# Attention kernel: diagonal blocks share PSUM banks, and the order of the work is laid out anew

## The reference, cut to what matters

```python
scores = jnp.einsum('bhqd,bhkd->bhqk', q, k) * scale
causal = jnp.tril(jnp.ones((t, t), dtype=bool))
scores = jnp.where(causal[None, None], scores, -jnp.inf)
att = jax.nn.softmax(scores, axis=-1)
y = jnp.einsum('bhqk,bhkd->bhqd', att, v)
```

## Time and profile before

| | |
|---|---|
| median of three runs | 1970.04 us (1965.76 to 1972.16) |
| the profiled execution | 1966.68 us |
| its span, first to last instruction | 1964.9 us |
| mean granted TensorE clock | 0.979 |
| PE busy | 1860.7 us, 95% |
| DVE busy | 1697.8 us, 86% |
| ACT busy | 1611.4 us, 82% |
| POOL busy | 554.1 us, 28% |

### The profile page before, as it was taken

How to read it: one execution, slowest core, us unless ns; L and a number is a source line. 1 busy time by engine, 2 the same in 40 slices (tenths; PEclk the granted TensorE clock), 3 DMA queues, 4 the chain that set the end, 5 groups by cost and what they waited for, 6 DMA issues and landing times.

```text
span 1964.9 us, 42229 instructions
## 1 busy us (share of the span) xinstructions
PE 1860.7 (95%) x13881; PEld 694.6 (35%) x13881; DVE 1697.8 (86%) x4770; ACT 1611.4 (82%) x2108; POOL 554.1 (28%) x712
## 2 busy tenths in 40 slices
PE   6899999999789999999999999999999999999998
PEld 6455565555322222222232322223232222223223
DVE  5699999999888898989899998989999899989861
ACT  2467666765269999999999999999999999999994
POOL 0112111221313424241442424143242414334211
PEclk8899999999769999999999999999999999999999
DMA  4133323335421404042341414133131414314012
GB/s 172 35 92 101 104 82 89 101 101 110 108 66 29 65 21 63 21 62 37 62 65 42 62 43 83 34 65 63 44 62 40 83 29 73 59 43 67 29 36 81
DMA packets 160327, 129.04 MB, mean 66 GB/s; under 512 B 95344, under 2 KB 144752, under 8 KB 159768
## 3 DMA queue, kind: packets, MB, share of 16 engines
q1 hardware_dynamic: 160152, 126.88, 30.0%
HBM read 74.60 MB, written 42.98 MB: 60 GB/s over the span
## 4 chain that ended last, share of the span: by engine, by line
PE 48%; ACT 16%; DVE 3%; issue 3%; DMA 2%; SPq 2%; POOL 1%; ACTq 0%; POOLq 0%; DVEq 0%
PE pv L1511 20%; ACT prob L1304 12%; PE st L1498 11%; PE sm L1477 10%; PE sm L1448 3%; ACT excess L1297 3%; PE st L1486 3%; DMA scratch_i<-inverse 1%; DVE pm L1383 1%; DVE sm L1379 1%; PE sm L1472 1%; SPq L913 1%; DVE sm L1368 0%; ACT Y L1287 0%; DMA Yc<-Y 0%
## 5 line engine op out<-in xcount | busy, mean ns | idle before, releaser
L1304 ACT ACTIVATE prob<-st 128x1024 f32<-128x1024 f32 (+3 forms) x1280 | 1078.3, 900 | 77.8 <-PE st L1498 66.1
L1511 PE MATMUL pv<-prob,V 128*32 128x512 f32 (+3 forms) x5120 | 594.1, 541 | 0.4 <-POOL prob L1261 0.2
L1368 DVE CUSTOM_DVE_ANT_0 sm<-sm,mask 128x128 f32<-128x128 f32 (+3 forms) x1024 | 491.6, 510 | 62.5 <-PE sm L1477 50.3
L1477 PE MATMUL sm<-K,Q 48*128 48x512 f16 (+3 forms) x2112 | 522.7, 349 | 16.3 <-DVE pm L1383 4.3
L1498 PE MATMUL st<-Q,K 50*128 50x512 f16 (+3 forms) x2560 | 484.1, 353 | 28.5 <-ACT prob L1304 21.1
L1261 POOL TENSOR_SCALAR_AFFINE_SELECT prob<-prob 128x256 f32<-128x256 f32 x512 | 206.1, 409 | 932.3 <-ACT prob L1304 926.5
L1383 DVE TENSOR_REDUCE pm<-sm 128x1 f32<-128x512 f32 x640 | 416.8, 683 | 24.3 <-PE sm L1477 22.1
L1379 DVE CUSTOM_DVE_ANT_0 sm<-sm,excess 128x512 f32<-128x512 f32 x448 | 311.1, 716 | 33.7 <-PE sm L1477 25.8
L1477 PEld LDWEIGHTS sm<-K,Q 48*128 48x128 f16 x2112 | 167.5, 94 | 324.9 <-DVE pm L1383 158.6
L1498 PEld LDWEIGHTS st<-Q,K 50*128 50x128 f16 x2560 | 126.6, 93 | 421.3 <-ACT prob L1304 299.6
L1297 ACT ACTIVATE excess<-st 128x1024 f32<-128x1024 f32 x219 | 224.8, 1026 | 17.6 <-PE st L1486 10.8
(11 more groups left out here) (171 smaller groups left out, 1939.0 us busy)
## 6 DMA issues: line engine op xcount, KB each, us to landing
Q<-scratch_q SPq DMA_DIRECT2D x102, 128.0 KB, 4.5
K<-scratch_k SPq DMA_DIRECT2D x102, 128.0 KB, 7.2
x<-in_x SPq DMA_DIRECT2D x16, 512.0 KB, 4.4
scratch_v<-Rt SPq DMA_DIRECT2D x64, 128.0 KB, 2.0
scratch_r<-Rt SPq DMA_DIRECT2D x16, 512.0 KB, 3.2
V_raw<-scratch_v SPq DMA_DIRECT2D x16, 512.0 KB, 10.1
Yc<-Y SPq DMA_DIRECT2D x124, 64.0 KB
spread<-scratch_i SPq DMA_DIRECT2D x124, 64.0 KB, 2.2
```

The source lines that it names most:

```text
L1304: act.activation(prob[(slot * UNITS + k) % PT][:, :, 0:width], st[number % ST][:, :, 0:width], ACT.Exp)\
L1368: dve.tensor_tensor_reduce(x, x, mask[:, CH - width:], 1.0, -3e38, ALU.add, ALU.max, pm[:, row, t, k:k + 1]).then_inc(sm_read, 1)
L1477: pe.matmul(dst[:, 0:block_width(t, k)], lhsT=Q[slot][r, h // 2, t * P:(t + 1) * P], rhs=K[slot][r, h // 2, k * CH:k * CH + block_width(t, ...
L1511: i = pe.matmul(pv[2 * DH * h:2 * DH * (h + 1), CH - width:CH], lhsT=V[quad % VSLOTS][:, j, h, :], rhs=prob[(slot * UNITS + 2 * n + h // 2 ...
```

## The change

- **Units.** For each `c` the first diagonal tile stays a full unit for each pair of heads. The second (384 queries) and the fourth (128) of a pair of heads now share one bank pair and one exponential, and the third tile (256) of both pairs of heads shares one. All 68 units of a quad are 1024 wide; there are 36 steps of weighted sums, of which the one with tiles 2 and 4 holds 16 matmul pieces for 8.
- **Masks.** A step with 384/128 takes four mask instructions, the 256/256 one takes one instruction over 4 x 128 elements.
- **Edges.** Two narrow edge blocks share an `sm` bank and one handover: 256 + 256 of the two pairs of heads, 128 + 384 of two row tiles of a head. 64 blocks in 40 entries; VectorE still has one instruction for each block. Both blocks of a bank are of one `g`.
- **Differences.** 12 for 14: the row tiles of `c` = 2 use one only for the first pair of heads. 24 paired and 48 plain entries.
- **Layout.** A new timetable of 235 letters (279 before), 119 entries, `AHEAD` 58, new places of the projections. The buffers `prob` are counted through over the quads, since 68 is no multiple of 8, and an exponential waits for the step that used its buffer last.

The core of the diff:

```diff
-PROJECT_AT = (78, 91, 107, 121)
+PROJECT_AT = (64, 77, 87, 99)
...
+def by_difference(c, hp, t):
+
+    return c == 3 or c == 2 and hp == 0
...
             for hp in range(G // 2):
-                pair = c == 3 or c == 2 and (hp == 0 or t % 2 == 1)
-                for k in range(c + 1):
+                pair = by_difference(c, hp, t)
+                for k in range(c):
                     if pair and k == 1:
                         continue
-                    role = "edge" if k == c else "paired" if pair and k == 0 else "plain"
-                    blocks += [(role, 2 * hp + g, t, k) for g in range(2)]
+                    role = "paired" if pair and k == 0 else "plain"
+                    blocks += [(role, ((2 * hp + g, t, k, 0),)) for g in range(2)]
+            pairs = range(G // 2)
+            if place == 1:
+                blocks += [("edge", tuple((2 * hp + g, t, c, hp * 2 * P) for hp in pairs)) for g in range(2)]
+            elif place == 2:
+                blocks += [("edge", ((2 * hp + g, t - 2, c, 0), (2 * hp + g, t, c, P))) for hp in pairs for g in range(2)]
+            elif place == 3:
+                blocks += [("edge", ((2 * hp + g, t, c, 0),)) for hp in pairs for g in range(2)]
...
-AHEAD = 73
+AHEAD = 58
...
+def score_units():
+
+
+    units, steps = [], []
+    for c in range(TC):
+        wide = [j for j in range(SUB * c + 1)]
+        for j in wide:
+            first = len(units)
+            units += [(c, ((hp, j, CH, 0),)) for hp in range(G // 2)]
+            steps.append((c, ((j, CH, ((first, 0), (first + 1, 0))),)))
+        d, first = SUB * c, len(units)
+        units += [(c, ((hp, d + 1, 3 * P, 0), (hp, d + 3, P, 3 * P))) for hp in range(G // 2)]
+        steps.append((c, ((d + 1, 3 * P, ((first, 0), (first + 1, 0))), (d + 3, P, ((first, 3 * P), (first + 1, 3 * P))))))
+        units.append((c, ((0, d + 2, 2 * P, 0), (1, d + 2, 2 * P, 2 * P))))
+        steps.append((c, ((d + 2, 2 * P, ((first + 2, 0), (first + 2, 2 * P))),)))
+    return units, steps
...
 TIMETABLE = (
...
-    "mmwmsmmswsmmmswmsmmsmswsmmmswmsmsmmwxmmswmmsmxmmwsmsmmwsmsmmxmmswsmm"
-    "s"
+    "mwmxmmswxmmsmmsmwmsmsmwmmsmswsmmxwmxmmsmmmsmswsmmmswsmsmmmsmmxmxmwxm"
+    "msmsmwxmmsmwsmmsmmmssmwmxmwmssmmwsmmmswsmmsmwsmmswmsmmxwsmsmmsmwsmms"
+    "mwsmsmmwxmmsmwmssmmwmsmwsmsmmwmmsmswmsmsmwsmsmmwsmmsmwsmmswmsmsmwmsm"
+    "mswmsmmswmsmmswmsmmswmsmxmwmsms"
 )
...
-                        if k % 2 == 0:
-                            act.wait_ge(pair_used, quad * PAIRS + k // 2 + 1)
+                        number, before = XAHEAD + NUMBERS[last][k], quad * UNITS + k - PT
+                        if before >= 0:
+                            act.wait_ge(pair_used, before // UNITS * STEPS + STEP_OF[before % UNITS] + 1)
                         act.wait_ge(st_ready, quad * UNITS_RUN + number + 1)
...
                 for a in both_halves():
                     r = slice(ROW * a, ROW * a + KD + 2)
-                    i = pe.matmul(st[number % ST][:, a, 0:width], lhsT=K[slot][r, u % 2, j * P:(j + 1) * P],
-                                  rhs=Q[slot][r, u % 2, (c + 1) * CH - width:(c + 1) * CH], start=True, stop=True)
+                    for hp, j, width, at in parts:
+                        i = pe.matmul(st[number % ST][:, a, at:at + width], lhsT=K[slot][r, hp, j * P:(j + 1) * P],
+                                      rhs=Q[slot][r, hp, (c + 1) * CH - width:(c + 1) * CH], start=True, stop=True)
                 i.then_inc(st_ready, 1)
```

More of the change, by code:

```diff
@@ L997, in attention, with prob_of @@
         I_v = scr["I"].rearrange("k h t -> k (h t)")
-        order = ORDER
-        diag = [j >= SUB * c for c, j, _ in order]
+        def prob_of(quad, u):
+            return prob[(quad * UNITS + u) % PT]
         def unit_done(quad, number):
@@ L1241, in body @@
-                for n, (c, j, width) in enumerate(order):
-                    if last and n == SUB * (TC - 1) * TC // 2 + SUB:
+                for n in range(STEPS):
+                    if last and n == STEP_AT[TC - 1] + SUB:
                         normalise_late(0)
-                    if last and n == sum(SUB * c for c in range(1, TC + 1)) - SUB:
+                    if last and n == STEP_AT[TC - 1] + SUB * (TC - 1):
                         normalise_late(1)
-                    if n == SUB * (TC - 1) * TC // 2 and quad and quad % 2 == 0:
+                    if n == STEP_AT[TC - 1] and quad and quad % 2 == 0:
@@ L1247, in body @@
                         normalise(quad - 1, 1)
-                    if n == SUB * (TC - 1) * TC // 2 + (2 if last else SUB + 2) and quad % 2:
+                    if n == STEP_AT[TC - 1] + (2 if last else SUB + 2) and quad % 2:
                         normalise(quad, 0)
-                    if n == SUB * 3 and not last:
+                    if n == STEP_AT[2] and not last:
                         turn, nxt = quad // SLOTS, (slot + 1) % SLOTS
                         difference_of_keys(quad + 1, nxt, (turn + (2 if nxt == 0 else 1)) * (16 * LOADS))
-                    if n == sum(SUB * c for c in range(1, TC)) and not last:
+                    if n == STEP_AT[TC - 1] and not last:
@@ L1264, in body @@
-                assert d == DIAG
+                        for x, count in diagonal_blocks(quad, n, u):
+                            pool.affine_select(out=x, in_=x, compare_op=ALU.is_ge, fill=0.0, base=0,
+                                               pattern=[[0, count], [1, P]], channel_multiplier=-1).then_inc(masked, 1)
             pool.memset(yn[:, :, :], 0.0).then_inc(yn_cleared, 1)
@@ L1282, in evac @@
             def evac(quad, c):
-                ends = sum(x[0] <= c for x in order)
-                act.wait_ge(pair_used, quad * PAIRS + ends + PT // 2)
+                act.wait_ge(pair_used, quad * STEPS + STEP_AT[c + 1])
                 if c % 2 == 0:
@@ L1299, in body @@
                     elif kind == "scores":
-                        number, width = XAHEAD + NUMBERS[last][k], order[k // 2][2]
-                        if k % 2 == 0:
-                            act.wait_ge(pair_used, quad * PAIRS + k // 2 + 1)
+                        number, before = XAHEAD + NUMBERS[last][k], quad * UNITS + k - PT
+                        if before >= 0:
+                            act.wait_ge(pair_used, before // UNITS * STEPS + STEP_OF[before % UNITS] + 1)
                         act.wait_ge(st_ready, quad * UNITS_RUN + number + 1)
[L1304 to L1307, removed]
+                        act.activation(prob_of(quad, k)[:, :, :], st[number % ST][:, :, :], ACT.Exp).then_inc(exp_done, 1)
+                    elif kind == "sums" and quad + ahead >= 0 and k + 1 in STEP_AT:
+                        evac(quad + ahead, STEP[k][0])
             for r in range(XAHEAD):
@@ L1500, in scores @@
                 i.then_inc(st_ready, 1)
             def weighted_sums(quad, slot, n, last):
-                c, j, width = order[n]
-                if j == 0:
+                c, blocks = STEP[n]
+                if n == STEP_AT[c]:
                     pe.wait_ge(pv_read, quad * TC + c + 1)
-                if diag[n]:
-                    pe.wait_ge(masked, quad * DIAG + 2 * sum(diag[:n + 1]))
-                else:
-                    pe.wait_ge(exp_done, unit_done(quad, NUMBERS[last][2 * n + 1]))
@@ L1510, in weighted_sums @@
-                for h in range(G):
-                    i = pe.matmul(pv[2 * DH * h:2 * DH * (h + 1), CH - width:CH], lhsT=V[quad % VSLOTS][:, j, h, :],
-                                  rhs=prob[(slot * UNITS + 2 * n + h // 2) % PT][:, h % 2, 0:width],
-                                  start=j == 0, stop=j == SUB * (c + 1) - 1, tile_position=(0, 2 * DH * h))
-                    if h == G - 1:
-                        i.then_inc(pair_used, 1)
+                if DIAGONAL[n]:
+                    pe.wait_ge(masked, quad * sum(MASKS) + sum(MASKS[:n + 1]))
+                else:
+                    pe.wait_ge(exp_done, unit_done(quad, NUMBERS[last][UNITS_OF[n][-1]]))
@@ new lines, in weighted_sums @@
+                for j, width, src in blocks:
+                    for h in range(G):
+                        u, at = src[h // 2]
+                        i = pe.matmul(pv[2 * DH * h:2 * DH * (h + 1), CH - width:CH], lhsT=V[quad % VSLOTS][:, j, h, :],
+                                      rhs=prob_of(quad, u)[:, h % 2, at:at + width],
+                                      start=n == STEP_AT[c], stop=n + 1 == STEP_AT[c + 1], tile_position=(0, 2 * DH * h))
+                i.then_inc(pair_used, 1)
@@ L1547, in _ @@
             quads(body)
-            for n in range(PAIRS - LAG, PAIRS):
+            for n in range(STEPS - LAG, STEPS):
                 weighted_sums(NQ - 1, (NQ - 1) % SLOTS, n, True)
```

96 lines of the change are left out of this document (54 added, 42 removed).

## The result

The changed kernel takes 2083.21 us (2080.43 to 2085.98), the kernel before 1971.1 us beside it: ratio 1.0565, 95% interval 1.0543 to 1.0586. That is 112 us slower where I forecast 37 us faster.

A forecast was written before the change was run, and what follows sets the result against it. A ring of ScalarE, VectorE and TensorE bounds it. Mean of ScalarE's 82.9 and VectorE's 84.1 us a quad, -3.1, plus 0.7 row wait: -2.4 over 16 quads, +1 at start: 1933 us (1918 to 1950; overall 1900 to 1970).

The forecast's parts named there:

- The step that failed: GpSimd's masks and long operations: hidden, priced at nothing; at the other end 0.7 us a quad.
- ScalarE at 82.9: ScalarE's period per quad if it sets the pace: 75.2 us of work plus 7.7 of loss, 3.7 less than before.
- the row wait: First score of the last column block waits for row-maxima DMAs: about 0.7 us a quad, bounds 0 and 2.
- ScalarE's loss: Time beyond its slot for each ScalarE instruction: 0.092 us, carried over to 84 instructions a quad.
- VectorE's term: VectorE's busy time a quad: 78.5 us plus 2.2 is 80.7; at 96% full, a period of 84.1 us.
- TensorE's same-half pieces: Matmuls sharing a bank follow each other on one row half: up to 2.5 us a quad, priced at nothing.
- My second rival: TensorE's order sets the pace at diagonal scores and edges: 2.5 us a quad slower, 2011 us; chance 0.08.
- Masks: New 256/256 mask: one GpSimd instruction of 512 elements for two of 256, between 0.41 and 0.82 us, hidden.
- Edges two to a bank: Row-maxima edges: 40 handovers for 64 cut VectorE's idle time before them, 4.0 us a quad, by up to 1.5.
- Differences and width: ScalarE per quad: two fewer `excess` passes save 1.8 us, exponentials all 1024 wide save 0.56 us.
- the fourth: Rival: gain lost to late rows, or masks with rows: 1953 us, 1965 with both; chance 0.09.

The follow-up runs named there:

- early chain: The changed kernel with GpSimd's key differences for the next quad made one column block earlier, before the second block's masks: 1920.53 us, ratio 0.9758.
- the alternated order: The early chain with pieces of shared score units issued alternately on the two row halves, not one half after the other: 1922.93 us, ratio 0.976.

## Why the prediction was wrong

- **The step that failed** is the one on GpSimd: "POOL is busy 32% and its long operations sit where they sat, so nothing". They do sit there. I looked at who waits behind them in GpSimd's own list, the masks, and not at who waits for what they make. The first difference of the next quad had moved from 20 to 5 ScalarE instructions behind the chain's start, with 13.1 us of chain: 13.1 - 5 = 8 us, and 7.8 were measured. The numbers for it were all in the trace of before and in the two timetables. I had made just this count, transpose to first score, for the row maxima, and for `DK` not.
- **The clock** was in none of my terms: a standstill of 8 us brought 2.2 us more in each quad, through the half clock.
- **The rest of the sum came out near, in part by luck.** Without the wait (early chain) a quad takes 83.1 us; I had 83.5 from ScalarE at 82.9 and VectorE at 84.1. 1920.5 us is inside my range, 13 under the forecast; the 0.7 us that I added for the row wait are 11 of them. ScalarE's loss for each of 84 instructions is (83.1 - 75.2)/84 = 0.094 us for the 0.092 that I carried over. VectorE's term was wrong in both of its parts. I read it as 90.6% busy, gives 90.3; and I added 2.2 us of busy time a quad, while it rose by 0.4, from 1083.88/13.86 = 78.2 to 1135.20/14.44 = 78.6 us, for my 80.7. Its idle time is 4.5 us a quad (8.4 before) where my 96% left 3.4. The two errors stand against each other.
- **The row wait** came as forecast (0.8 us for 0.7, once a quad), and taking it away gains nothing. Wrong in the sum, right as an event.
- **TensorE's same-half pieces** at nothing: right for the scores, by the alternated order; untested for the edges. My second rival (2011 us by TensorE's order) has no part in the slowdown, since the early chain has the same pieces in the same order and takes 1920.5 us: the rival had the right sign for another reason.
- **Masks**: the new form takes 0.64 us for 512 elements, inside 0.41 to 0.82, and is hidden.
- **Edges two to a bank**, "up to 1.5 us a quad": mis-sized. VectorE's idle time before edges fell by 2.5 us, from 4.0 a quad to (11.4 + 0.1 + 8.9 + 1.2)/14.44 = 1.5 in the early chain. Undone on this timetable the sharing costs 84 us, 5 a quad; I take the depth of the banks for its main worth, with the reservations above.
- **Differences and width**: I had 1.8 us for the two `excess` passes and 0.56 for the width; undone, they cost 44 us (2.8 a quad, with misplaced letters) and 5.7 us (0.35).
- **Rivals.** None named this wait. The nearest in words was the fourth, a gain lost in a wait of the new layout, with 0.09 and the wrong wait in it.

## What to carry to other kernels

When a schedule is laid out anew, list every product that crosses engines with the place where it is begun, its length and its first reader, and count the distance anew for each, above all for engines that look idle: GpSimd was idle for 67% of the time, and that did not help a chain of 13 us with a reader 5 us away. In an in-order ring one early reader stops everybody, and its standstill is paid again through the clock. Moving the producer up was the cheapest cure here: one line was worth 163 us.

## What I had not expected of the hardware

Each standstill of TensorE of 7.8 us is followed by some 5 to 8 us at half clock, and 60 matmuls without use, which fill most of it, bring 33 us: kept at work through the wait, TensorE does what comes behind it faster. And the order of single instructions in a full ring counts as well as their sum: one `x` moved behind eight letters costs 14 us, 0.7%, with all counts, banks and semaphores the same.
